# A token mixer's state space scan: in place on the forces, drive matmuls among the last two units, first half fixed ahead of the second's carries, a finer wait

## The reference, cut to what matters

```python
s = 1.0 / (1.0 + dt * dt * a)
Bu = jnp.einsum('bnq,pq->bnp', u, W_B) + b_B
f_x = dt * s * Bu
f_z = dt * dt * s * Bu
def step(carry, f):
    x, z = carry
    fx, fz = f
    x_new = s * x - dsa * z + fx
    z_new = ds * x + s * z + fz
    return ((x_new, z_new), z_new)
...
x = einsum(y, W_C) + b_C + (einsum(u, W_D) + b_D)
x = jax.nn.gelu(x, approximate=False)
out = x * jax.nn.sigmoid(x) + u
```

## Time and profile before

| | |
|---|---|
| median of 3 runs | 997.69 us (995.52 to 999.02) |
| the profiled execution | 993.78 us, its span 991.7 us |
| PE busy | 896.9 us, 90% of the span |
| DVE busy | 763.6 us, 77% |
| ACT busy | 498.8 us, 50% |
| POOL busy | 436.8 us, 44% |
| mean granted PE clock | 0.985 |

### The profile page before, as it was taken

How to read it: one execution, slowest core, us unless ns; L and a number is a source line. 1 busy time by engine, 2 the same in 40 slices (tenths; PEclk the granted TensorE clock), 3 DMA queues, 4 the chain that set the end, 5 groups by cost and what they waited for, 6 DMA issues and landing times.

```text
span 991.7 us, 24234 instructions
## 1 busy us (share of the span) xinstructions
PE 896.9 (90%) x9608; PEld 375.7 (38%) x9608; DVE 763.6 (77%) x1293; ACT 498.8 (50%) x767; POOL 436.8 (44%) x259
## 2 busy tenths in 40 slices
PE   4799999999999999999999988596989989989996
PEld 1234344343443434434344343232333433433333
DVE  4687887878878878788787868996677677677675
ACT  3545454454544545445454413366656556555552
POOL 3577676776766767767676610000110110110000
PEclk9999999999999999999999999797999999999999
DMA  9468878788787887878878560000000000000000
GB/s 370 124 182 242 260 216 253 222 241 263 211 251 224 240 263 212 248 228 240 266 207 250 147 161 11 0 1 1 1 11 22 11 12 22 12 11 18 16 12 32
DMA packets 49060, 141.62 MB, mean 143 GB/s; under 512 B 5440, under 2 KB 5440, under 8 KB 40768
## 3 DMA queue, kind: packets, MB, share of 16 engines
q1 hardware_dynamic: 48960, 140.17, 47.7%
HBM read 68.85 MB, written 4.19 MB: 74 GB/s over the span
## 4 chain that ended last, share of the span: by engine, by line
PE 79%; DVE 12%; issue 3%; ACT 3%; DMA 1%; POOL 1%; SPq 0%; DVEq 0%; POOLq 0%; ACTq 0%
PE ring L821 21%; PE bank_ms L793 11%; PE qp L858 11%; PE bank_sq L793 6%; PE ring L1030 4%; DVE sb_prodv L1201 4%; PE ring L1004 3%; PE bank_ms L1042 3%; DVE sb_arena L417 2%; PE bank_sq L1030 2%; PE qp L992 2%; PE bank_ms L1037 1%; PE ring L955 1%; PE ring L1011 1%; DMA sb_arena<-x 1%
## 5 line engine op out<-in xcount | busy, mean ns | idle before, releaser
L821 PE MATMUL ring<-sb_arena,sb_wqkv 64*64 64x512 f32 x2048 | 267.8, 606 | 21.4 <-DVE sb_prodv L1201 19.0
L1201 DVE TENSOR_TENSOR sb_prodv<-ring,sb_wbc 128x1024 f32<-128x1024 f32 x128 | 154.2, 1207 | 33.3 <-PE ring L821 31.1
L1170 DVE TENSOR_TENSOR sb_prodk<-ring,sb_qbuf 128x1024 f32<-128x1024 f32 x128 | 153.3, 1220 | 18.2 <-PE ring L821 15.5
L446 POOL TENSOR_TENSOR sb_rows<-sb_arena 128x2048 f32<-128x2048 f32 x31 | 141.8, 4575 | 15.9 <-DMA sb_arena<-x 15.8
L563 POOL TENSOR_TENSOR sb_parts_q<-sb_arena,sb_const 128x512 fp32r<-128x512 f32 x15 | 15.7, 1044 | 297.0 <-ACT sb_arena L680 297.0
L858 PEld LDWEIGHTS qp<-sb_prodv,sb_tok_w 64*64 64x64 f32 x4096 | 119.7, 133 | 53.8 <-issue 50.4
L858 PE MATMUL qp<-sb_prodv,sb_tok_w 64*64 64x128 f32 x4096 | 128.4, 269 | 2.5 <-DVE sb_prodv L1201 2.5
L603 ACT ACTIVATE sb_xsq<-sb_arena 128x2048 f32<-128x2048 f32 x64 | 118.4, 1897 | 9.2 <-DMA sb_arena<-x 9.2
L821 PEld LDWEIGHTS ring<-sb_arena,sb_wqkv 64*64 64x64 f32 x2048 | 58.7, 132 | 154.5 <-issue 81.4
L419 ACT ACTIVATE sb_arena<-ring,sb_rest_w 128x512 f32<-128x512 f32 x120 | 82.2, 686 | 42.6 <-PE ring L1004 17.6
L529 POOL TENSOR_TENSOR sb_score<-sb_score,sb_smx 128x512 f32<-128x512 f32 x32 | 41.0, 1281 | 83.1 <-DVE sb_smx L1184 78.7
(11 more groups left out here) (202 smaller groups left out, 1405.8 us busy)
## 6 DMA issues: line engine op xcount, KB each, us to landing
sb_arena<-x SPq DMA_DIRECT2D x64, 1024.0 KB, 8.5
sb_wbc<-sb_wgt SPq DMA_DIRECT2D x256, 256.0 KB, 5.6
out<-sb_arena SPq DMA_DIRECT2D x16, 256.0 KB, 2.0
sb_rest_w<-rest_w SPq DMA_DIRECT2D x1, 918.5 KB, 21.7
sb_const<-const SPq DMA_DIRECT2D x1, 264.5 KB, 3.0
sb_tok_w<-tok_w SPq DMA_DIRECT2D x1, 260.5 KB, 2.9
sb_const<-const SPq DMA_DIRECT2D x1, 256.0 KB, 21.7
```

The source lines that it names most:

```text
L446: eng.tensor_tensor(rows[:, :, :, :], pix[:, :, 0:8], pix[:, :, 8:16], ALU.add).then_inc(sum8_ready, 1)
L821: mm = pe.matmul(ring[slot][C * half:C * half + C, i, :], image_block(w, i), x[C * i:C * i + C, m, half, c], start=True, stop=True)
L1170: dve.tensor_tensor(by_pixel(prodk[:, c]), by_pixel(ring[c % 2][:, :, :]), q[:, :, None, :].to_broadcast([P, 2, N_PIX, G32]), ALU.mult).th ...
L1201: dve.tensor_tensor(prodv[:, :, :, G32 * c:G32 * (c + 1)], by_pixel(ring[k % 2][:, :, :]), by_pixel(wbc[:, c]), ALU.mult).then_inc(values_ ...
```

## The change

1. `drive(0, ...)` for the first half was four pieces ahead of the values of unit 31 and four behind them. Now piece 0 stands between the values of unit 30, and a new function `last_step` spreads the rest over unit 31. ACT's `forcing(0)` is not split any more.
2. The scan works in place: forces of half 0 lie in `arena[:, 0:HP]`, those of half 1 in `wbc`, the scan writes over them, gelu and silu too. `scan_first` and its copies are gone, and the semaphore counts fall by one.
3. `EARLY` falls from 6 to 5 and `BEFORE_TOKENS` from 12 to 9.
4. The 16 `fix_z(0, j)` stand ahead of the carries of half 1, no longer between them.
5. `centre_rows(i)` waits for `i * 2 * N_RES // ITERS + 1` pieces of the residual, and the waits for whole halves go. `norm_sq(0)` stands behind the first silu of half 1 instead of the second.
6. The experts' buffers move: `mix` begins at `arena[:, HP:]`, `h1e` lies in `prodk`.

```diff
-        mix = arena[:, :]
+        mix = arena[:, HP:]
...
-        h1e = cut(8 * CH).rearrange("p (m e n) -> p m e n", m=2, e=E)
+        h1e = prodk[:, :, :, :].rearrange("p e m n -> p m e n")
...
-        force = arena[:, 0:2 * HP]
-        z = arena[:, 2 * HP:4 * HP]
+        z = (arena[:, 0:HP], wbc[:, :, :, :].rearrange("p c b n -> p (c b n)"))
...
                 if not nxt:
-                    forcing(0, range(4))
+                    forcing(0)
...
             pipeline(act, step, UNITS)
-            forcing(0, range(4, N_PIECE))
...
-                    if h == 1 and n == N_RES - 2:
+                    if h == 1 and n == 1:
                         norm_sq(0)
...
                 if nxt:
                     scores(n + 1)
-                else:
-
-                    pe.wait_ge(rest_in, 16)
-                    pe.wait_ge(variance_ready, UNITS)
-                    pe.wait_ge(scores_scaled, UNITS)
-                    pe.wait_ge(tokens_ready, UNITS // 2)
-                    drive(0, range(4))
                 values(n, m, 0)
...
                 if nxt2:
                     query(n + 2, m2)
+                elif nxt:
+                    pe.wait_ge(rest_in, 16)
+                    pe.wait_ge(variance_ready, UNITS)
+                    drive(0, range(0, 1))
                 values(n, m, 2)
...
-            for n in range(UNITS):
+            def last_step(n, m):
+                pe.wait_ge(scores_scaled, UNITS)
+                drive(0, range(1, 3))
+                values(n, m, 0)
+                for part in range(4):
+                    project(n - 1, part)
+                values(n, m, 1)
+                drive(0, range(3, 4))
+                values(n, m, 2)
+                values(n, m, 3)
+                drive(0, range(4, 6))
+                for part in range(4):
+                    project(n, part)
+                drive(0, range(6, N_PIECE))
+
+            for n in range(UNITS - 1):
                 step(n, n % NF)
-            drive(0, range(4, N_PIECE))
-            for part in range(4):
-                project(UNITS - 1, part)
+            last_step(UNITS - 1, (UNITS - 1) % NF)
...
                 pe.wait_ge(normed_ready, i)
-                if i == ITERS // 2:
-                    pe.wait_ge(residual_ready, 2 * N_RES)
+                pe.wait_ge(residual_ready, i * 2 * N_RES // ITERS + 1)
...
-            pe.wait_ge(residual_ready, N_RES)
             pe.wait_ge(gelu_ready, 2 * N_PIECE)
...
-            def scan_first(h):
-                dve.wait_ge(force_ready, N_PIECE * h + 1)
-                dve.tensor_copy(z[:, at(h, 0)], force[:, at(h, 0)]).then_inc(scan_step[h], 1)
-
             def scan_ahead(h, j):
...
-                dve.wait_ge(scan_step[h], 2 * j - 1)
+                if j > 1:
+                    dve.wait_ge(scan_step[h], 2 * j - 2)
...
-            EARLY, BEFORE_TOKENS = 6, 12
+            EARLY, BEFORE_TOKENS = 5, 9
...
             for j in range(L):
-                if j < NCK - 1:
-                    carry_from(1, j)
                 fix_z(0, j)
-                if j < NCK - 1:
-                    carry_to(1, j)
+            for c in range(NCK - 1):
+                carry_from(1, c)
+                carry_to(1, c)
```

More of the change, by code:

```diff
@@ L356, in build, with at, piece @@
         ctmp = xsq[:, 4 * CH:4 * CH + 2 * PAIRS]
-        def at(h, j):
-            return slice(h * HP + j * HS, h * HP + (j + 1) * HS)
-        def piece(h, n, size=CH):
-            return slice(h * HP + n * size, h * HP + (n + 1) * size)
+        def at(j):
+            return slice(j * HS, (j + 1) * HS)
+        def piece(n, size=CH):
+            return slice(n * size, (n + 1) * size)
         def tokens_at(h, n, steps):
@@ L647, in forcing @@
                     act.wait_ge(drive_mm, N_PIECE * h + n + 1)
-                    act.activation(force[:, piece(h, n)], drive_banks[n % 2][:, :], ACT.Identity,
+                    act.activation(z[h][:, piece(n)], drive_banks[n % 2][:, :], ACT.Identity,
                                    scale=sv[:, SV_F:SV_F + 1], bias=sv[:, SV_FB:SV_FB + 1]).then_inc(force_ready, 1)
@@ L689, in _ @@
                     act.wait_ge(mixed_mm, N_PIECE * h + n + 1)
-                    act.activation(force[:, piece(h, n)], banks[n][:, :], ACT.Gelu,
+                    act.activation(z[h][:, piece(n)], banks[n][:, :], ACT.Gelu,
                                    bias=sv[:, SV_CD:SV_CD + 1]).then_inc(gelu_ready, 1)
@@ L694, in _ @@
                 for n in range(N_RES):
-                    if h == 1 and n == N_RES - 2:
+                    if h == 1 and n == 1:
                         norm_sq(0)
-                    a = force[:, piece(h, n, HP // N_RES)]
+                    a = z[h][:, piece(n, HP // N_RES)]
                     act.activation(a, a, ACT.Silu).then_inc(silu_ready, 1)
@@ L941, in _ @@
                         pe.wait_ge(v_share_ready, 2 * n + 2)
-                        pe.matmul(banks[n][:, :], wssm[:, 1, :], v_share[:, piece(0, n)], start=False, stop=False)
+                        pe.matmul(banks[n][:, :], wssm[:, 1, :], v_share[:, piece(n)], start=False, stop=False)
                     pe.wait_ge(chunk_fixed[h], fixed(h, 2 * n + 1))
-                    pe.matmul(banks[n][:, :], wssm[:, 1, :], z[:, piece(h, n)],
+                    pe.matmul(banks[n][:, :], wssm[:, 1, :], z[h][:, piece(n)],
                               start=False, stop=True).then_inc(mixed_mm, 1)
@@ L1210, in tokens @@
                                          ALU.add, ALU.add).then_inc(tokens_ready, 1)
-            def scan_first(h):
-                dve.wait_ge(force_ready, N_PIECE * h + 1)
-                dve.tensor_copy(z[:, at(h, 0)], force[:, at(h, 0)]).then_inc(scan_step[h], 1)
             def scan_ahead(h, j):
-                dve.wait_ge(scan_step[h], 2 * j - 1)
+                if j > 1:
+                    dve.wait_ge(scan_step[h], 2 * j - 2)
                 if j + 1 < L:
                     dve.wait_ge(force_ready, N_PIECE * h + (j + 1) // 2 + 1)
-                    dve.scalar_tensor_tensor(force[:, at(h, j + 1)], z[:, at(h, j - 1)], sv[:, SV_NS:SV_NS + 1],
-                                             force[:, at(h, j + 1)], ALU.mult, ALU.add).then_inc(scan_step[h], 1)
+                    dve.scalar_tensor_tensor(z[h][:, at(j + 1)], z[h][:, at(j - 1)], sv[:, SV_NS:SV_NS + 1],
+                                             z[h][:, at(j + 1)], ALU.mult, ALU.add).then_inc(scan_step[h], 1)
             def scan_on(h, j):
-                dve.wait_ge(scan_step[h], 2 * j - 1)
-                dve.scalar_tensor_tensor(z[:, at(h, j)], z[:, at(h, j - 1)], sv[:, SV_G:SV_G + 1], force[:, at(h, j)],
+                if j > 1:
+                    dve.wait_ge(scan_step[h], 2 * j - 2)
+                dve.scalar_tensor_tensor(z[h][:, at(j)], z[h][:, at(j - 1)], sv[:, SV_G:SV_G + 1], z[h][:, at(j)],
                                          ALU.mult, ALU.add).then_inc(scan_step[h], 1)
@@ L1247, in carry_from @@
             def carry_from(h, c):
-                dve.wait_ge(scan_step[h], 2 * L - 1)
+                dve.wait_ge(scan_step[h], 2 * L - 2)
                 dve.wait_ge(carry_step[h], 4 * c + 2)
-                for o, (coef, loc) in enumerate(((cz, z[:, at(h, L - 1)]), (cv, seqs(vel, h)))):
+                for o, (coef, loc) in enumerate(((cz, z[h][:, at(L - 1)]), (cv, seqs(vel, h)))):
                     dve.scalar_tensor_tensor(tmp(h, o), start(seqs(zin, h), c), coef[:, L, 0:1], start(loc, c),
@@ L1332, in residual @@
                     dst = tokens_at(h, n, L // N_RES)
-                    out = force[:, piece(h, n, HP // N_RES)].rearrange("p (j n) -> p j n", n=HS)
+                    out = z[h][:, piece(n, HP // N_RES)].rearrange("p (j n) -> p j n", n=HS)
                     dve.scalar_tensor_tensor(dst, dst, 2.0, out, ALU.mult, ALU.add).then_inc(residual_ready, 1)
@@ L1340, in _ @@
             scan_last(0)
-            scan_first(1)
             for j in range(1, L):
```

13 lines of the change are left out of this document (6 added, 7 removed).

## The result

| | before | after |
|---|---|---|
| first comparison, median | 997.35 us (8 executions) | 989.79 us (8) |
| second | 993.88 us (12) | 989.70 us (6) |
| third | 994.08 us (9) | 989.54 us (5) |
| profiled execution, its span | 993.78, 991.7 us | 989.44, 986.7 us |
| mean granted clock of TensorE | 0.985 | 0.987 |

What follows compares the result with a forecast made beforehand. It took VectorE and TensorE to bound different stretches, TensorE the last before the final gelu. Terms -7.6+2.75+2.7-1.05 = -3.2 us, put on the 997.69 us median, gave 994.5 us, range 990.8 to 998.2.

Steps and rivals of the forecast that it cites:

- The pause that hides piece 0: TensorE, before unit 30's last values: piece 0 takes 1.12 us in a 1.17 us pause, price nothing, 1.1 us at most.
- the new waits in unit 31: VectorE's products of unit 31 wait for spread transfers: 3.4 us of new waits, products ending at 599.4.
- steps of 1.58 us on TensorE: Mixing of half 1: each piece waits for four fixes, 1.58 us, of which TensorE works 0.86.
- in place worth nothing: Scan of half 0: two copies go; the first lay inside a wait, the second is worth 0 to 0.29 us, taken as 0.
- Rival C: TensorE at half rate while mixing half 1, a piece taking 1.72 us: gain 1.2, total 996.5 us; chance 15%.
- Rival D: TensorE's clock at half before project(31), tokens of unit 31 at 607.7 instead of 603.2: slower, 999.0 us; chance 10%.
- the base of 997.69 us: Median of the runs of the kernel before, from which the forecast took the gain of 3.2 us.
- landings: Spread transfers of unit 31: third lands 6.0 us after issue, at 593.1, seventh 5.5 us after, at 597.0.
- lone carry: VectorE, half 1: a carry without a fix beside it takes 0.99 us, 14.9 us for fifteen; bounds 0.81 and 1.2.
- Rival B: Unit 31: transfers don't hold the products, which start at 591.3; gain 6.5, total 991.2 us; chance 12%.
- 2.7 us longer: VectorE, scan_last(1) to the fixes of half 1: 21.7 us instead of 19.0 with fixes ahead of carries.
- Finer wait, "worth nothing": centre_rows(0) still waits for the last gelu: no gain, up to 1 us lost if the square had to wait.

Runs made afterwards that it cites:

- e3: Kernel before with the front part alone: new TensorE order and fewer early scan steps, copies, alternating fixes and coarse waits kept; 989.95 us, ratio 0.9945.
- e8: Changed kernel with unit 31's spread transfers issued chunk by chunk instead of alternately; 989.45 us.
- e6: Changed kernel with the finer wait undone, TensorE waiting for all four residual steps of half 0 again; 989.33 us.
- e4: Kernel before with one part alone, all fixes of half 0 ahead of the carries of half 1; 996.88 us, ratio 1.0017.
- e13: Kernel before with three unread products filling TensorE's 3.2 us pause between the second and third value of unit 31; 994.99 us, ratio 0.9998.
- e9: Changed kernel with two scan steps in the wait before unit 31's third product and drive piece 6 ahead of the last projection; 987.95 us, ratio 0.992.

## Why the prediction missed

**Right.** The pause that hides piece 0, the first scan step (586.45 for 586.7), the new waits in unit 31, the 16 fixes in a row, VectorE as the new limit, steps of 1.58 us on TensorE, gelu 1.3 us behind the last fix, in place worth nothing (e3 keeps the copies: 30.8 us against 30.4 to 30.9, and 21.4 between the two scan_last in both). Rival C, half rate while half 1 is mixed, did not happen: granted clock 1.00 from 655.7 to 670.6, with 0.46 us of waiting ahead of each of five pieces. The Trainium skill, "TensorE: Matmul & The Clock Gate", section on a second HAM failure mode (HAM is its name for what gates the clock), tells of a clock that swings at frequent short idles, seen in a bf16 kernel; in this stretch of fp32 products it did not show. Rival D did not happen either: project(31) took 3.72 us.

**The steps that failed** are two sizes, not the mechanism: the base of 997.69 us (below), and in the sum the landings and the lone carry. On the profiles the last gelu comes 4.95 us earlier, not 3.2.

- *Landings.* I took 6.0 and 5.5 us from issue to landing out of the earlier trace rows; they were 5.1 and 5.0, and the seventh was issued 0.3 us sooner. It goes beyond these two profiles: in the three profiles of the changed kernel the third took 4.9 to 5.3 us and the seventh 4.6 to 5.6, in the seven of before both took 5.5 to 6.0. Why, no run shows. Products start at 592.18 and 596.29, not 593.2 and 597.05, and scan_last(0) comes at 609.54 instead of 610.25: **0.7 us**. Rival B, that landings don't hold the products, is refuted: the seventh landed at 591.17+5.0 = 596.2, and the product starts at 596.29 behind 1.75 us of waiting; in e8 the landings move and the products with them. That B's 991.2 lies nearer to the measured time than my number is luck. The eighth transfer, issued at 592.09, landed 4.8 us later, at 596.9, when the DMA engines had been all but idle since 596.0 (busy 0.71 from 595.5 to 596, 0.02 from 596 to 597). The rule that the semaphore waits for the receipt (the Trainium skill, "DMA: Bandwidth & Descriptors", the anatomy of one DMA) fits that delay; that it is the receipt, no run shows.
- *The lone carry.* Priced 0.99 us from the gaps, measured 0.93: the gap from carry_from to carry_to is 0.27 (637.85 to 638.12), not 0.35. That 0.35 was read at the last carry of half 0, and the changed kernel has it there too; why it is longer there stays open. With the rest, scan_last(1) to the fixes of half 1 took 651.64-630.98 = 20.7 us instead of 21.7: **1.0 us**. The term "2.7 us longer" was 1.7.
- *Finer wait, "worth nothing".* Worth 0.65 us beside the fixes-first order, whose loss it repairs (e6, e4); with the old order 0.4 to 0.5 in two profiles of nine. In the sum it made no difference, since I had not charged that loss.

**The base.** These explain 1.75 us. The prediction then put the profile's difference on 997.69, the median of three runs. That was the wrong place: the kernel before has medians of 993.9 to 996.0 in the five other comparisons and 994.9 over all 100 executions. 994.9-3.2 would have been 991.7, inside the range; 997.69-4.95 = 992.7 would have been inside it too. It took both errors to leave it: of the miss of 4.7 us to 989.8 some 2.8 are the base and some 2 the terms. The profile at 993.78 was no odd execution (the other six took 992.22 to 996.34); it was the three runs that lay high. Why the kernel before takes over 997 us in a fifth of its executions stays open; two of ten executions of e9, at 993.3 and 993.6 us, lie as far above their median, so the new order is not free of it for certain.

**What the profile of before hid.** Its distance to scan_last(0), 36.05 us, is on the lower of two levels. Against the mean of seven the front part gives 6.1 us, 0.6 more than against the first, and the one profile of e13 puts about 2 of them down to TensorE's half rate behind the 3.2 us pause. By the means: -6.1 in front, +0.6 for the fixes first, -0.1 in the wait, together -5.6, beside -5.3 in the medians.

## What to carry to other kernels

Price each part of a change by itself and let the front part stand alone once: here one part gave everything, one cost 0.6 us, and one only repaired a second cost of that one. A chain of small dependent operations hides its hand-overs best with one filler in each gap, not with all fillers ahead of it. When the profiled execution and the median differ by more than the effect, take the base from more executions before adding a difference to either.
